# Sum of the values over all keys: three tiles added on GpSimd ahead of one product with the constant matrix

## The reference, cut to what matters

```python
q = (x @ Wq.T + bq).reshape(B, S, N_HEADS, D_K)
k = (x @ Wk.T + bk).reshape(B, S, N_HEADS, D_K)
v = (x @ Wv.T + bv).reshape(B, S, N_HEADS, D_K)
scores = jnp.einsum('bqhd,bkhd->bhqk', q, k) * SCALE
scores = jnp.where(mask, scores, jnp.float32(-10000.0))
attn = jax.nn.softmax(scores, axis=-1) + jnp.float32(1e-09)
ctx = jnp.einsum('bhqk,bkhd->bqhd', attn, v).reshape(B, S, D_MODEL)
return ctx @ Wo.T + bo
```

## Time and profile before

| | |
|---|---|
| median of 3 runs | 2509.32 us (2508.38 to 2514.21) |
| the profiled execution, its own time | 2514.33 us |
| its span | 2512.5 us |
| mean granted TensorE clock | 0.937 of full speed |
| busy: PE, PEld, DVE, ACT, POOL | 87%, 67%, 54%, 45%, 34% |

### The profile page before, as it was taken

The page is one execution under the profiler, slowest core; times in us unless marked ns, Lnnn a source line. Parts: engine busy times, 40 slices in busy tenths (PEclk is TensorE's granted clock), DMA queues, the critical chain, the costliest instruction groups (busy, mean ns, idle before and its releaser), DMA issues.

```text
span 2512.5 us, 44998 instructions
## 1 busy us (share of the span) xinstructions
PE 2178.1 (87%) x13718; PEld 1676.1 (67%) x13812; DVE 1354.5 (54%) x3491; ACT 1119.0 (45%) x2511; POOL 855.1 (34%) x1549
## 2 busy tenths in 40 slices
PE   3679898898988989989899898987577998998997
PEld 2346665666665666656666666654377998998997
DVE  2446555565555555555556555554265555646654
ACT  0235444444454444544444444442134654554553
POOL 3011222232232323232222322233255445545544
PEclk7689999999999999999999999997788999999999
DMA  3210211202112021020120211100133223233222
GB/s 126 51 35 17 57 33 37 56 6 56 38 32 56 9 59 42 22 56 23 46 53 10 56 29 40 44 8 13 57 95 107 46 42 74 48 71 73 41 45 42
DMA packets 89697, 116.31 MB, mean 46 GB/s; under 512 B 23718, under 2 KB 76262, under 8 KB 87334
## 3 DMA queue, kind: packets, MB, share of 16 engines
q1 hardware_dynamic: 66294, 87.89, 12.5%
q0 software_dynamic: 23360, 27.91, 6.7%
HBM read 51.56 MB, written 26.71 MB: 31 GB/s over the span
## 4 chain that ended last, share of the span: by engine, by line
PE 53%; issue 14%; SPq 12%; DVE 8%; DMA 4%; ACT 4%; POOL 4%; DVEq 0%; POOLq 0%; ACTq 0%
PE ps L1674 9%; SPq L451 8%; PE ps L1534 6%; PE ps L1466 4%; SPq L447 4%; PE ps L1453 4%; PE ps L1685 3%; PE ps L1686 3%; PE ps L1687 3%; PE ps L1444 2%; PE ps L1373 2%; PE ps L1399 2%; PE ps L1571 2%; DMA xg<-xn_rows,idx_s 2%; PE ps L1445 1%
## 5 line engine op out<-in xcount | busy, mean ns | idle before, releaser
L1048 DVE TENSOR_REDUCE mx<-ps 128x2 f32<-128x512 f32 (+1 forms) x384 | 229.7, 599 | 391.8 <-PE ps L1445 329.1
L755 ACT ACTIVATE pT<-ps 128x512 f32<-128x512 f32 (+1 forms) x384 | 202.7, 528 | 415.1 <-PE ps L1453 412.5
L763 ACT ACTIVATE prob<-ps,mx 128x256 f32<-128x256 f32 (+1 forms) x768 | 294.2, 441 | 145.5 <-DVE mx L1048 136.4
L860 ACT ACTIVATE hid_hi<-ps,b 128x256 fp32r<-128x256 f32 x408 | 208.0, 510 | 164.5 <-PE ps L1674 151.8
L1444 PE MATMUL ps<-ks,qs 96*128 96x512 f32 (+1 forms) x384 | 198.9, 518 | 93.1 <-DMA ks<-k_lo 59.2
L1316 DVE TENSOR_TENSOR hid_lo<-hid_full,hid_hi 128x256 fp32r<-128x256 f32 x408 | 179.0, 448 | 151.0 <-ACT hid_full L863 145.9
L1685 PE MATMUL ps<-w_hi,hid_hi 128*128 128x256 f32 x816 | 237.4, 291 | 4.0 <-DVE hid_lo L1316 4.0
L1466 PE MATMUL ps<-pT,vaug 128*32 128x128 f32 x2560 | 220.5, 286 | 19.0 <-ACT pT L755 9.7
L1686 PE MATMUL ps<-w_lo,hid_hi 128*128 128x256 f32 x816 | 232.4, 285 | 0.0
L1687 PE MATMUL ps<-w_hi,hid_lo 128*128 128x256 f32 x816 | 232.0, 284 | 0.0
L1453 PE MATMUL ps<-ident,prob 128*128 128x128 f32 x1280 | 210.6, 280 | 16.2 <-ACT prob L763 9.3
(11 more groups left out here) (258 smaller groups left out, 4521.3 us busy)
## 6 DMA issues: line engine op xcount, KB each, us to landing
w_raw<-in_w SPq DMA_DIRECT2D x16, 1024.0 KB
xin<-in_x SPq DMA_DIRECT2D x32, 384.0 KB
qs<-q_hi SPq DMA_DIRECT2D x128, 96.0 KB, 2.2
ks<-k_hi SPq DMA_DIRECT2D x256, 48.0 KB, 2.1
qs<-q_lo SPq DMA_DIRECT2D x64, 96.0 KB, 2.2
ks<-k_lo SPq DMA_DIRECT2D x128, 48.0 KB, 2.1
xn_rows<-xc SPq DMA_DIRECT2D x16, 384.0 KB, 2.6
result<-h SPq DMA_DIRECT2D x16, 384.0 KB, 2.5
```

The lines of the kernel that those rows point to most:

```text
L763: ins = act.activation(prob[:, s % PB, hh, w], ps[:, s % 2, hh * 2 * P + w.start:(hh + 1) * 2 * P], ACT.Exp, bias=mx[:, s % 2, hh:hh + 1])
L860: act.activation(hid_hi[:, f], ps[:, f % 4, 0:CHUNK], ACT.Gelu_apprx_tanh, bias=b1[half][:, f:f + 1])
L1048: dve.tensor_reduce(mx[:, s % 2], sc, AX_X, ALU.max, negate=True).then_inc(max_done.sem, 1)
```

## The change

Before, TensorE multiplied each of the three value tiles with `ones9` and added the three results up in PSUM. After it, GpSimd adds the three value tiles element by element into a new tile `vsum` (two additions, the second waits for the first), and TensorE multiplies `vsum` with `ones9` once. GpSimd's two additions for batch b + 1 stand in its sequence b between `shared_residual(b-1)` and `chain_deviations(b, 0)`. They wait for `v_ready` of batch b + 1, and for the product of the batch before, which reads the same tile.

```diff
+        vsum = room("vsum", [P, NH, DK])
...
+        vsum_step = signal("values_half_summed", 1)
+        vsum_ready = signal("values_summed", 1)
...
+            def tiles_sum(b):
+
+                pool.wait_ge(v_ready.sem, v_ready.at(b, 1))
+                pool.wait_ge(sumv_done.sem, sumv_done.at(b, 0))
+                pool.tensor_tensor(vsum[:], vaug[:, 0, :, 0:DK], vaug[:, 1, :, 0:DK], ALU.add).then_inc(vsum_step.sem, 1)
+                pool.wait_ge(vsum_step.sem, vsum_step.at(b, 1))
+                pool.tensor_tensor(vsum[:], vsum[:], vaug[:, 2, :, 0:DK], ALU.add).then_inc(vsum_ready.sem, 1)
...
                 if chain:
                     chain_deviations(b - 1, 2)
                     shared_residual(b - 1)
+                if head:
+                    tiles_sum(b + 1)
                 if att:
                     chain_deviations(b, 0)
                 if head:
...
             head_deviations(0)
             residual(0)
+            tiles_sum(0)
             pool.wait_ge(slots_cleared.sem, slots_cleared.at(0, 48))
...
             def values_sum(b):
 
-                pe.wait_ge(v_ready.sem, v_ready.at(b, 1))
+                pe.wait_ge(vsum_ready.sem, vsum_ready.at(b, 1))
                 pe.wait_ge(h1_ready.sem, h1_ready.at(b, 0))
-                for i in range(NT):
-                    ins = pe.matmul(ps[:, 5, D:2 * D].rearrange("p (h d) -> p h d", h=NH), ones9[:], vaug[:, i, :, 0:DK],
-                                    start=(i == 0), stop=(i == NT - 1))
-                ins.then_inc(sumv_done.sem, 1)
+                pe.matmul(ps[:, 5, D:2 * D], ones9[:], vsum[:].rearrange("p h d -> p (h d)"), start=True, stop=True
+                          ).then_inc(sumv_done.sem, 1)
```

## The result

The changed kernel takes 2527.97 us in the median of 4 runs (2523.70 to 2530.44), beside 2511.03 us for the kernel before on the same chip (2508.38 to 2514.21, 4 runs). The ratio is 1.0065 with a 95% interval of 1.0045 to 1.0085: slower by 0.65%. I had forecast 2515 with a range up to 2526. The time lies above the range, nearest to rival (b).

A forecast was written before the change was run, and what follows sets the result against it. SyncE's copies were taken to end last at the seam, leaving TensorE room. Terms 0 - 2 + 0 + 0 + 7.7 = +5.7 us on the median 2509.3 gave 2515.0 us, range 2506 to 2526.

The forecast's parts named there:

- rival (b): TensorE's lower clock lasts two terms at 13 of 14 seams, 1.56 us each: +18.3 us, 2527.6 us; chance 0.18.
- What bounds the seam: At the seam between sequences SyncE's copies end last, releasing unit 3's scores; TensorE has room, 0.98 us of slack.
- Unit 3 still released by the DMA in every steady seam: Sign to check: unit 3 waits for the last pair's DMA, 3.9 us behind unit 1, in all steady seams.
- The product: TensorE's constant-matrix product at the seam: 0.86 us saved per batch, 0 on the ordinary path, -2 us from other seams.
- The additions: GpSimd's two additions ahead of `chain_deviations`: 0.77 us each, covered by GpSimd's idle time, direct cost 0.
- The shared port: GpSimd's second addition delays VectorE's copy L1084 and its chain by 0.6 us per seam, hidden: 0 on the path.
- The clock: TensorE's clock falls to half at 10 of the 11 seams that hold today, 0.77 us each: +7.7 us.
- the price of one fall: Cost of one clock fall at a seam: 0.77 us, from one pitch of 103.37 against 102.60.
- The bound of 1.7: Upper cost of one clock fall: work on the path behind unit 3 halved for about 3.4 us, costing 1.7 us.

The follow-up runs named there:

- h1: Changed kernel with the product executed twice, plus products for nobody: three in slot 7, two before unit 0, two behind it; 2487.09 us, ratio 0.9904.
- h3: Kernel before (three real products, no additions) with the same products for nobody as h1; 2490.65 us, ratio 0.9903.
- e3: Changed kernel keeping the additions and the wait, but multiplying the three value tiles as before, the added tile unused; 2511.28 us, ratio 1.0009.
- e1: Changed kernel with the single product executed three times, each writing the same sum; 2511.39 us, ratio 1.0004.
- e2: Changed kernel with the single product executed twice; 2507.41 us, ratio 0.9993.
- h2: Changed kernel, product once, with two products for nobody before unit 0 and two behind it, nothing in slot 7; 2510.34 us, ratio 0.9998.
- e4: Kernel before with the product of the first value tile alone and no additions, so sums are incomplete; 2533.25 us, ratio 1.0081.
- g1: Changed kernel with the product executed twice and three products for nobody in slot 7 from batch 2 on; 2489.28 us, ratio 0.9909.
- g2: Kernel before with three products for nobody in slot 7, made of the first value tile; 2489.44 us, ratio 0.9915.

## Why the prediction was wrong, by its own steps

- **What bounds the seam**: right. SyncE's copies of the last pair still end last there when TensorE keeps its clock. In h1, at 1.00, unit 3's scores still wait for the DMA:

```profile
482.61 0.38 PE L1471 MATMUL ps<-ks,qs 96*128 96x256 f32 x1 [0.45 <-DMA ks<-k_lo]
...
486.50 0.38 PE L1471 MATMUL ps<-ks,qs 96*128 96x256 f32 x1 [1.04 <-DMA ks<-k_lo]
```

  The second row is unit 3, the first unit 1: 486.50 - 482.61 = 3.89 us apart, as in the kernel before (492.33 - 488.43 = 3.90). "Unit 3 still released by the DMA in every steady seam", though, went too far: in the long low stretch TensorE is busy with its own work until 909.23, and the chain goes through TensorE. Unit 3 starts no later for it (909.33 - 905.40 = 3.93); the loss lies behind it.
- **The product, 0 on the path in ordinary seams, -2 in others**: the zero is shown by h1 against h3. In batches 0 and 1 nothing came back: from the first projection to the third the changed kernel took 189.5 us (63.3 to 252.8) and the one before 188.8 (68.8 to 257.6). At a seam with a short fall time did come back: 5.62 - 4.90 = 0.72 us at the seam, and 0.57 in the pitch (102.80 for 103.37), of the 0.77 that I had set as the most. The new falls cost many times that.
- **The additions, 0**: right. 0.73 us each (I took 0.77), no penalty for strided reads, and e3 within 0.3% of before.
- **The shared port, 0.6 us, hidden**: the size was 0.36 (0.919 for 0.559 us), hidden by e1 and e3. The Trainium skill, "SBUF — State Buffer", section "Who interferes with whom", has, for a VectorE copy in a two-port mode, the second operation blocked until the first is done. The direction agrees: the copy started at 896.41, behind the addition at 896.19, and was the one that took longer. The size does not quite: the addition had 0.50 us left (to 896.91), and the copy took 0.36 longer.
- **The clock, +7.7**: the term that failed. The direction was right, and that the clock brings it: e1, e2 and h2 bring the time back with work for nobody, e4 brings the loss without the additions. The number of falls was short by one (I said ten more of eleven; all 11 fell, and the three of before stayed). The price was off: I took 0.77 us a fall, and the loop lost 18.8 us, 1.45 a pitch above the mean before, which held its own falls already. In the alternating part the falls come in two kinds. A short one ends before unit 3 and costs 0.2 us (102.80). A long one, 10.2 us, costs 2.8 (105.43), nearly twice rival (b)'s 1.56. (b) named the mechanism of the long one, work behind unit 3 at 1.2 GHz, but put it at 13 of 14 seams; they alternate, which the chain shows and no step of mine foresaw. That its 18.3 us come close to the 16.9 measured is luck: its price was too low for the long ones and too high for the short.
- The step that failed is therefore the price of one fall, 0.77 us, read from a single pitch of before. That pitch, 103.37, held a fall whose low stretch ended at 698.30, ahead of unit 3's scores. Of its 0.77 us, 0.72 arose between unit 1's scores and the router's product, where the three products ran at half speed on the path, and this the change takes away. What the new falls cost is something else: the work behind unit 3 at half speed, 1.86 us for a stretch of 3.4 us there, 2.7 for one of 6.8 us that reached into it (pitch 105.27), 2.8 for one of 10.2. The bound of 1.7 was too low, since it allowed one stretch of 3.4 us alone.
- The Trainium skill, "TensorE: Matmul & The Clock Gate", section "A second HAM failure mode: psum-queue depth-cycling", was listed as speaking against the change. The traces agree that the clock swings between its two levels: to 0.50 and back at all 14 seams.

Why the two kinds alternate is open: I did not vary the length of a sequence by itself. So is why filling the rank stage made more seams fall (11 of 14 in g1 and g2). The extra 4 to 5 us of e4 over the changed kernel (1.0081 against 1.0065, intervals overlap) do not lie in the steady loop, whose mean pitch is 104.17 in e4 and 104.39 in the changed kernel; they lie before and behind it. Of the 8.8 us between the two profiled spans 5.9 are the later start of the very first projection (69.2 against 63.3).

## What to carry to other kernels

An engine's work that lies in a wait is not free to remove when that engine's clock depends on its being busy: read the granted clock of the stretch before taking matmuls out of it. Where TensorE waits for others in each turn of a loop and the clock falls there, products for nobody in the wait can pay: about 1.3 us of them in slot 7 brought the mean pitch from 102.94 to 101.75 us (g2). Then look at the other places again, since more of them may fall than before (g1, g2). Price a fall by the work on the path that it can reach, not by one row that shows one, and ask whether that row's price is made of the very work that the change removes.

## What I had not expected of the hardware

The kernel before was itself slowed in 13 of 14 sequences by a fall in the rank stage, and it ran 0.9% faster with three products for nobody a sequence, without the change (g2) or with it and the product twice (g1). The alternation in the changed kernel was steady for its last nine pitches (105.4 and 102.8, each within 0.05 us); that one fall's delay decides how the next seam falls is likely, but only argued. GpSimd's addition of 16 columns out of every 32 took 0.728 to 0.732 us, no more than that of contiguous rows (0.723 to 0.778).
